# Four reorderings and four empty instructions in a two-layer attention and mixer kernel on one Trainium2 core

## The reference

```python
x = x + _L0_attn_ref(_layernorm(x), Wq, Wk, Wv, Wo, Wg, Win, ...)   # decayed linear attention, 32 heads, 8 k/v heads
x = x + _L0_ffn_ref(_layernorm(x), router_weight, ...)              # top 8 of 64 router, adds mixed bias rows
x = x + _L1_attn_ref(_layernorm(x), in_proj_w, conv_w, ...)         # state-space mixer, 128 heads in 8 groups
x = x + _L1_ffn_ref(_layernorm(x), A, B, Wr)                        # top 16 of 64 rank-16 adapters
```

```python
# attention: decay rows exp(G_i - G_j) per head, gate = x @ Wg.T, y = y / rms * gnorm_w * silu(gate)
# mixer: dt = clip(softplus(dt + dt_bias)), A_cum = cumsum(dt * A)
hBC = silu(conv(x @ in_proj_w))            # hs, B, C
xch = hs * dt[..., None]                   # the scaled input
Y_diag = einsum(C, B, exp(segsum(A_dt)), xch)
Y = Y_diag + Y_off + hs * D                # then y * silu(gate), group norm, out_proj
```

## Time and profile before

| what | value |
|---|---|
| median of 3 runs | 2616.07 us (2611.06 to 2619.6) |
| the profiled execution's own time | 2612.99 us |
| its span, first to last instruction | 2611.3 us |
| PE busy | 2486.1 us, 95% of the span |
| DVE, ACT, POOL busy | 1849.1, 1499.3, 1540.3 us |
| attention phase, about | 42 to 880 us of the span |
| middle phase, about | 880 to 1034 us |
| mixer phase, about | 1034 to 2500 us |

### The profile page before, as it was taken

One profiled execution on the slowest core, in us unless ns is written; L12 is line 12 of the kernel. 1 busy time (PEld: TensorE's weight loads), 2 busy tenths in 40 slices (PEclk: granted clock), 3 DMA queues, 4 the chain that ended last, 5 costly groups with the idle time before them and its releaser, 6 DMA issues.

```text
span 2611.3 us, 60268 instructions
## 1 busy us (share of the span) xinstructions
PE 2486.1 (95%) x19326; PEld 2011.8 (77%) x19326; DVE 1849.1 (71%) x2688; ACT 1499.3 (57%) x3416; POOL 1540.3 (59%) x1495
## 2 busy tenths in 40 slices
PE   5999999999999788999999999999999999999989
PEld 4788788788787667787787777777778877877777
DVE  4776766757767777777777687687777777786864
ACT  3535435445445465765765775676667657756721
POOL 1655656546546341767667576686676676676710
PEclk8999999999999999999999999999999999999999
DMA  4031220320321025323222322232232222222111
GB/s 113 28 81 36 61 76 21 80 68 20 85 46 43 28 93 164 102 67 102 100 78 76 102 93 74 87 104 89 68 109 90 72 97 99 78 82 95 58 41 49
DMA packets 93597, 199.32 MB, mean 76 GB/s; under 512 B 11248, under 2 KB 19440, under 8 KB 93296
## 3 DMA queue, kind: packets, MB, share of 16 engines
q1 hardware_dynamic: 93296, 195.64, 24.4%
HBM read 184.46 MB, written 11.14 MB: 75 GB/s over the span
## 4 chain that ended last, share of the span: by engine, by line
PE 47%; issue 4%; DVE 3%; POOL 3%; ACT 2%; DMA 0%; ACTq 0%; DVEq 0%; POOLq 0%; SPq 0%
PE proj L210 11%; PE proj L212 10%; PE proj L211 10%; PE core_y L1635 3%; PE core_o L1641 2%; PE turned L1665 1%; PE mx_normed L1665 1%; PE mx_decay L210 1%; PE turned L245 1%; PE core_y L212 1%; PE core_y L210 1%; PE mx_decay L212 1%; PE mx_decay L211 1%; PE core_y L211 1%; DVE slab_lo L193 1%
## 5 line engine op out<-in xcount | busy, mean ns | idle before, releaser
L193 DVE TENSOR_TENSOR slab_lo<-slab_raw,slab_hi 128x512 fp32r<-128x512 f32 (+2 forms) x256 | 252.8, 999 | 156.1 <-ACT slab_hi L184 133.8
L210 PE MATMUL proj<-slab_hi,XTL 128*128 128x512 f32 x816 | 348.2, 427 | 1.4 <-DVE at_ropeB L841 0.9
L210 PE MATMUL proj<-XTH,slab_lo 128*128 128x512 f32 x716 | 292.8, 409 | 34.0 <-DVE at_ropeB L841 13.0
L212 PE MATMUL proj<-slab_hi,XTH 128*128 128x512 f32 x816 | 319.9, 392 | 0.0
L211 PE MATMUL proj<-slab_lo,XTH 128*128 128x512 f32 x816 | 319.0, 391 | 0.0
L212 PE MATMUL proj<-XTH,slab_hi 128*128 128x512 f32 x716 | 286.6, 400 | 9.8 <-issue 9.8
L211 PE MATMUL proj<-XTL,slab_hi 128*128 128x512 f32 x716 | 284.7, 398 | 0.0
L1922 POOL TENSOR_TENSOR mx_gate<-mx_gate,mx_hd 128x512 f32<-128x512 f32 x128 | 170.5, 1332 | 137.0 <-DVE mx_hd L1830 125.7
L210 PE MATMUL proj<-slab_hi,mx_otl 128*128 128x512 f32 x576 | 240.6, 418 | 2.0 <-DVE mx_otl L259 2.0
L906 POOL TENSOR_TENSOR at_ropeA<-at_ropeA,at_ropeB 128x512 f32<-128x512 f32 x80 | 110.2, 1378 | 204.7 <-DVE at_ropeB L841 204.7
L212 PE MATMUL proj<-slab_hi,mx_oth 128*128 128x512 f32 x576 | 227.6, 395 | 0.0
(11 more groups left out here) (414 smaller groups left out, 6684.1 us busy)
## 6 DMA issues: line engine op xcount, KB each, us to landing
mx_g_all<-sums SPq DMA_DIRECT2D x128, 512.0 KB, 3.7
at_g_all<-sums SPq DMA_DIRECT2D x64, 256.0 KB, 8.2
slab_raw<-in_w_gate SPq DMA_DIRECT2D x64, 256.0 KB, 3.1
slab_raw<-in_w_out SPq DMA_DIRECT2D x64, 256.0 KB, 3.0
slab_raw<-in_w_x SPq DMA_DIRECT2D x60, 256.0 KB, 4.9
slab_raw<-in_w_q SPq DMA_DIRECT2D x32, 256.0 KB, 3.1
slab_raw<-in_w_g SPq DMA_DIRECT2D x32, 256.0 KB, 8.6
slab_raw<-in_w_o SPq DMA_DIRECT2D x32, 256.0 KB, 3.1
```

What stands on the lines that cost most here:

```text
L193: op = nc.vector.tensor_tensor(K.SL[par][:, c, 0:width], K.RAW[c][:, 0:width], hi, ALU.subtract)
L210: nc.tensor.matmul(to[:, 0:bh.shape[-1]], al, bh, start=(c == 0), stop=False)
L212: mm = nc.tensor.matmul(to[:, 0:bh.shape[-1]], ah, bh, start=False, stop=(c == KC - 1))
```

## The change

1. In attention, SP loads the gate slab (slab 2) ahead of the eight decay rows; before it came behind them. The output slab (slab 3) stays behind them.
2. In the middle phase, POOL makes the low parts of slab BC+2 ahead of the last two decay steps.
3. In the middle phase, the turn of q moves from unit 20 to 18 and that of R from 24 to 26; that of G stays at 22. ACT's copies move with them.
4. In the mixer, POOL makes the scaled input first in its slot, ahead of the sum, the gate product and the tiny steps.
5. Four empty instructions stand on PE just ahead of the mixer's loop.

```diff
@@ attention, sync
                 for c in range(KC):
                     load_slab(sp, n + 1, 1, g, c)
+                for c in range(KC):
+                    load_slab(sp, n + 2, 2, g, c)
                 sp.wait_ge(S["at_e"], HEAD + PAIRS * g)
...
-                for j in (2, 3):
-                    for c in range(KC):
-                        load_slab(sp, n + j, j, g, c)
+                for c in range(KC):
+                    load_slab(sp, n + 3, 3, g, c)
@@ middle phase
-    SCAN_AT, Q_AT, G_AT, R_AT, STORE_AT = 14, 20, 22, 24, 15
+    SCAN_AT, Q_AT, G_AT, R_AT, STORE_AT = 14, 18, 22, 26, 15
@@ middle phase, gpsimd
         nc.gpsimd.tensor_tensor(G[:, :], e[:, :], q[:, :], ALU.subtract).then_inc(vv, 1)
+        lows(BC + 2)
         pool.wait_ge(vv, HEAD + 4)
...
-        for n in range(BC + 2, BC + 5):
+        for n in range(BC + 3, BC + 5):
             lows(n)
@@ mixer phase
     POOL_SILU = 6
+    LOOP_PAD = 4
@@ mixer phase, tensor
+            for _ in range(LOOP_PAD):
+                pe.nop(nofuse=True)
             with pe.Fori(0, G1 - 1) as g:
@@ mixer phase, gpsimd
+                    if r in SCORE1:
+                        t = SCORE1.index(r)
+                        pool.wait_ge(S["mx_hs"], HEAD + NT * q + 4 * (t // 4 + 1))
+                        pool.wait_ge(S["mx_y"], HEAD + NT * q + t - 1)
+                        alone(pool)
+                        nc.gpsimd.tensor_tensor(XCH[t % 2][:, :, :], HS[:, t, :].rearrange("p (h n) -> p h n", h=HH1),
+                                                bc(dtk[:, t, heads], [P, HH1, P1]), ALU.mult).then_inc(S["mx_xc"], 1)
                     if r in YSLOT:
...
                         hs = HS[:, t, :].rearrange("p (h n) -> p h n", h=HH1)
-                        pool.wait_ge(S["mx_hs"], HEAD + NT * q + 4 * (t // 4 + 1))
-                        pool.wait_ge(S["mx_y"], HEAD + NT * q + t - 1)
-                        alone(pool)
-                        nc.gpsimd.tensor_tensor(XCH[t % 2][:, :, :], hs, bc(dtk[:, t, heads], [P, HH1, P1]), ALU.mult).then_inc(S["mx_xc"], 1)
```

## The result

The changed kernel takes **2591.18 us** in the median of 4 runs (2589.19 to 2593.05), the kernel before 2615.14 us in the median of 4 (2611.06 to 2619.6). The ratio is 0.991, with a 95% interval from 0.9893 to 0.9928. That is faster by 24 us; the forecast was 17 us, 2599 us, with a range from 2585 to 2610. The profiled execution took 2593.05 us with a span of 2591.3, against 2612.99 and 2611.3.

What follows compares the result with a forecast made beforehand. PE, busy for 95% of the span, was taken as the bound, leaving about 125 us idle to win. The terms -9.5 - 0 - 3.3 - 8 + 3.8 made -17 us, so 2616.07 became 2599 us, range 2585 to 2610.

Steps and rivals of the forecast that it cites:

- Part 1: Attention, gate slab ahead of the rows: round 0 gains 7.6 us, the other rounds 1.9; -9.5 us in all.
- The rows: Attention: decay rows issued behind the gate slab still land before ACT reads them, 8 us to spare; cost zero.
- Part 2: Middle phase, low parts ahead of two decay steps: PE's 5.2 us wait goes, but alone this gains 0.
- Part 3: Middle phase, turns further apart: G turned 4.2 us earlier; -3.3 us taken, between 2.7 and 4.2, ends -1 and -5.
- DVE's chain: Middle phase: 13 tiles at 2.26 us each plus pauses limit part 3, ending at 1029.4 against 1032.1 us.
- Part 4: Mixer, scaled input first on POOL: 1.0 us of each 1.4 us wait won in eight groups; -8 us.
- Part 5: Mixer, four empty instructions: each loop return's wait moves to the fourth matmul; +3.8 us, from 0 to +9.
- (d): Mixer loop: the empty instructions are dropped on the way to the chip; 2595 us, chance 0.08, inside the main case.
- Rival (a): Mixer: four instructions carry the loop's top over a packet's end, the sixth-matmul wait goes; 2582 us, chance 0.15.
- The sum: Whole kernel: the five parts add to -17 us, taking the median from 2616.07 to 2599 us.
- (b): Whole kernel: only round 0 and part of the rest pay; -6.6 us, 2609.5 us, chance 0.17.
- (c): Attention, slot 12 of each round: the rows become the bound and the kernel is slower, 2631 us; chance 0.04.

Runs made afterwards that it cites:

- pad_2_turns: The changed kernel with two unread 128x128 transposes in place of the four empty instructions; 14.4 us under the kernel before, ratio 0.9925 to 0.9962.
- changed_again: The changed kernel, unaltered, timed once more beside the kernel before on another chip; 16.4 us under the kernel before, ratio 0.9914 to 0.9954.

## Why the prediction was right, and where it was wrong

- **Part 1**, -9.5: measured -7.9. The wait of 5.1 and the half clock behind it went as said, 7.6. The 1.9 us more from the other seven rounds did not come: the small waits for the rotation are 7.9 and 8.9 us with the edit, 8.8 without. The estimate that two longer waits of ACT would show at PE was wrong; the small end of that step was the right value. Its large end was added wrongly: 7.6 and half of 8.8 make 12, not 13.
- **The rows**, 8 us to spare: measured 11. They are asked for 27.7 us ahead of the first read (364.12, 391.83), as reckoned (373 and 400.8), and need at most 16.5 us where I had up to 19. That all eight are waited for as one (L764) had been left open; the sum went by the last landing, which is the right one.
- **Part 2**, 0 by itself: measured 0, and the wait went where I said. That it is worth 1.5 us behind part 3 was not spelled out, but it was inside the -3.3 for the two.
- **Part 3**, -3.3 between 2.7 and 4.2: with part 2, -3.8. G is turned 5.7 us earlier in the phase, not 4.2 (984.23 less 873.16 is 111.1 after the phase's start, and 1000.13 less 883.37 was 116.8), and 1.9 of it is lost behind it. But not by DVE's chain, as the prediction had it: PE waits for nobody there, and the clock halves behind the wait of 3.6 us. So this number came out in part by luck. The sum for DVE's chain was also short: 13 times 2.26 is 29.4, not 28.9.
- **Part 4**, -8: measured -8.8. The scaled input is never waited for, as said. The remainder in the second halves is 0.2 us and not 0.45, and the first halves lost their waits for the addition too, so PE's waits at the product fell by 13.1 us (14.8 to 1.7). Of this the new small waits took back 5.7: DVE's gate 3.2, mx_otl 1.6 more (3.6 against 2.0) and the masked decay 0.9. The 7.4 that are left are what the changed kernel's mixer won in its profile. The forecast had none of these terms; that it came so near is in part luck.
- **Part 5**, +3.8: measured 0, and this is the step that failed: "What they do is to shift the loop in PE's list." Written as they are, they shift nothing. The case stood as (d) with a chance of 0.08. The reasoning on the packet's end was right and the runs with real instructions show it: four moved the wait by two matmuls, twelve removed it. Its size came out by the medians (4.3 us for four instructions); the one profile has 8.9, near my end of +9, with the clock down at five of six returns and not at two. Rival (a)'s price was off too: removing the wait gives 6.4 to 7.0 us and not 13, since POOL's first tile is late next. I had asked what is late next for every part but this.
- **The sum**: -7.9, -3.8, -8.8 and 0 make -20.5, against -17 forecast; without part 5 my sum was -20.8. That the two sums agree is partly luck, as parts 3 and 4 show. The result of 2591 is 8 us from the forecast, of which 3.8 are part 5; I take the rest for the scatter between comparisons: the second one gave 16.4 us, on the other side.
- **Rivals (b) and (c)** did not come. (b) had its 7.6 right for part 1 and was wrong for parts 3 and 4.

## What to carry to other kernels

Of two waits of an engine in a row, the second can hide the first: removing the first alone moved its 5.2 us into the second and won nothing, removing the second alone won 2.3 us, and both 3.8. Before the order on a slower engine is changed, read which wait is next and how long it will be.

A loop too long to be held costs a stand at each return, and where the second one falls depends on where the loop's top lies in the list of instructions; look at which matmul waits for "issue", and at the number of instruction packets. If a loop is to be shifted, check in the instruction count that the filler is there. Then ask who is late once the stand is gone: here POOL took back about half.

## What the runs showed of the hardware

An empty instruction of PE with no wait had no record and no place in the list (60268 instructions with and without the four). With a wait, long fulfilled, ahead of it the two had one record and one place: 60284 with sixteen of each. At which step on the way to the chip the empty ones go was not tried.

The wait at a packet's end behind a return is 1.2 to 1.9 us at the sixth matmul in the changed kernel and up to 2.25 at the fourth in pad_2_turns. Shifting the loop by twelve instructions took 6 of 148 packets away.

The loop of attention has 1108 records on PE. In the kernel before no instruction packet of PE moves from 152 to 760 us, where all six returns to its top lie, and each branch back takes 0.2 us. The loop of the mixer has 3732, and in the changed kernel its branch back takes 3.3 to 3.9 us at each of six returns, ahead of the stand at the sixth matmul.

Within the sixteen matmuls behind a return, matmuls 0.43 us apart instead of 0.23 are found at five of six returns in pad_2_turns, at two of six in the changed kernel and at none in changed_again. The last two are one kernel, and their mixers are 2.5 us apart (1466.7 and 1464.2).
